# The fifth tile of each sender block holds two slot pairs instead of four slots

## The chip, the cores and the metric

One Trainium2 chip, one of its cores. The metric is the device time of one execution in microseconds (us); lower is better. A core has five engines with a queue each: PE (TensorE, matmuls), DVE (VectorE), ACT (ScalarE), POOL (GpSimd, which here issues the indirect DMAs) and SP (SyncE, which issues nearly all other DMAs). They meet through semaphores; 16 DMA engines move the data.

## The reference, cut to what matters

A graph network of four parts over 3125 nodes and 53125 edges, width 128, each part followed by a residual and a layer norm:

```python
x = layernorm(x + gated_gnn(x))     # 2 steps: msgs = (h @ edge_W[type])[src]; sum by dst; GRU
x = layernorm(x + rgcn(x))          # 3 layers: mean by (type, dst) of x[src], a weight per type, relu
x = layernorm(x + gcn(x))           # sum by src of norm[src] * norm[dst] * x[dst], one weight
x = layernorm(x + mlp(concat([x, mean_by_src(edge_attr), mean_by_dst(edge_attr)])))
```

All of it is gather by one end of an edge and sum by the other.

## The kernel before

**Slots and records.** The 25 blocks of 126 sender nodes (`TB`, `BS`) each get a run of slots, one for every edge that the block sends; an edge's slot is its rank in its block. Four slots in a row are one record of 4 x 128 floats in the DRAM tensor `chunks` (`x1_d`), and a code (target and type) for each of the four stands behind them. 128 records are a tile. A block has `QS` = 5 tiles, so `CAP` = 2560 slots, and there are `NQ` = 125 tiles.

**First loop** (52 groups of 1024 edges). It computes the first message sum and, beside it, each edge's rank: `ranks` on DVE turns a rank into a lane (`slot_lane`) and a column (`slot_col`); ACT builds the one-hot columns from `slot_col` (line 1364), DVE the lanes (`lanes_of`), and PE places the edges (line 892) in a table of slots. The ACT queue also hands POOL the row numbers of a later group (line 1344) for its gathers.

**Layers 1 to 4** (k = 1 is the second GNN step, 2 to 4 the RGCN layers) have two kinds of work. A *tile*: DVE compares the senders' lanes with the lane number (`shot`, `slot_hot`), PE multiplies it with the block's rows, one matmul a slot, four a tile (line 1030, `spread_slots`), ACT evacuates to one of `XS` = 6 buffers `xs` (line 1386, `keep_tile`), and SP stores that buffer into `chunks` (line 601, `store_tile`); before every fifth tile's store or behind it SP loads the lanes of a block three ahead. A *window* (149 of 21 target nodes): POOL gathers 128 records (line 735) into `rec`, DVE compares the codes (`dhot`), and PE sums by target and type (line 1058). In layer 1 all tiles come first, then all windows; POOL copies each tile's codes into `xs` and SP stores them with the tile. In layers 2 to 4 a plan written out by `joined` interleaves them: tiles go block by block within a round, the fourth slot group of all blocks before the fifth, so tiles 100 to 124 are the fifth tiles of the 25 blocks, the *last round*, with 36 to 38 windows between them. POOL waits for the stores of a round before the first window that needs it, and between its gathers it also scatters the edges' attributes (line 744), two in three windows of layers 3 and 4. The layers' order is fixed, so what SP issues is in the order of `store_tile`.

**GCN stage** (the last one). Now the sum goes by sender: SP loads one tile's records and its attributes into one of `GR` = 6 buffers `grec` (lines 720 and 721, two DMAs a tile, the first waits until the matmuls of the tile six before are done), DVE makes `ghot` (`slot_hots`), PE multiplies, four matmuls a tile (line 1289), and after each block of five tiles the sums are turned (`turn`, three matmuls). The tiles go block by block here, so every fifth is a fifth tile.

A float32 matmul shows in the profile as two records of the line. Layer norms, the GRU and the MLP lie between and after these stages.

## Time and profile before

| | before |
|---|---|
| timed runs, median of 3 (range) | 2967.55 us (2962.49 to 2968.0) |
| profiled execution, span | 2969.2 us |
| PE busy, share of the span | 2492.2 us (84%) |
| DVE | 1808.3 us (61%) |
| POOL | 1585.9 us (53%) |
| ACT | 868.5 us (29%) |
| stores of a tile (layer 1 / 2 to 4) | 258 KB x125 / 256 KB x375, one DMA each |
| loads of a tile in the GCN stage | 256 KB and 32 KB, x125 each |

The profile is of one execution, whose own time is its span, 1.7 us over the median of the timed ones. PE's share is an average over stages with different limits: slices of the span stand between 50% and 99% busy. In the profile's rows, a line Lnnn is a line of the kernel, x is a count, and SPq is the issue of a DMA by SP (not counted as busy time).

### The profile page before, as it was taken

What the parts mean: (1) busy time and instruction counts of PE and PEld (TensorE: products, weight loads), DVE (VectorE), ACT (ScalarE), POOL (GpSimd) and SP (SyncE); (2) the same over time, 40 slices, a digit from 0 to 9 for tenths busy, and PEclk for the clock granted to TensorE, in tenths of its full rate; (3) what the DMA queues carried; (4) which work ended last, traced back from release to release, by engine and by line L of the source; (5) the groups of instructions that cost most, each with busy time, mean ns of one, the idle gap of its engine ahead of it and who ended that gap; (6) DMA issues with size and microseconds to landing.
All of it is one profiled execution on the core that took longest, in us unless ns stands there. A gap on an engine that the chain in (4) does not pass through costs nothing.

```text
span 2969.2 us, 45704 instructions
## 1 busy us (share of the span) xinstructions
PE 2492.2 (84%) x15625; PEld 2211.7 (74%) x15625; DVE 1808.3 (61%) x6126; ACT 868.5 (29%) x1546; POOL 1585.9 (53%) x1706
## 2 busy tenths in 40 slices
PE   7587878888687899746999998998989897878798
PEld 3366666666387889436999997888988886777797
DVE  4565656575576777423876655676865554433585
ACT  2355555554354111213222231111311110443102
POOL 0656666663577666542566626666456665565200
PEclk9789888888799999857999999999999999898899
DMA  7312112110398666106888887877788774565793
GB/s 273 111 50 53 51 51 53 51 52 25 103 281 260 166 173 170 38 27 210 274 272 270 269 266 231 240 228 211 238 273 251 226 234 134 174 213 198 232 267 105
DMA packets 271515, 520.11 MB, mean 175 GB/s; under 512 B 61999, under 2 KB 115554, under 8 KB 270501
## 3 DMA queue, kind: packets, MB, share of 16 engines
q1 hardware_dynamic: 185053, 289.49, 31.2%
q0 software_dynamic: 86224, 227.59, 26.6%
q8 instruction: 132, 2.16, 0.3%
q14 instruction: 106, 0.87, 0.1%
HBM read 323.93 MB, written 192.99 MB: 174 GB/s over the span
## 4 chain that ended last, share of the span: by engine, by line
PE 69%; issue 10%; DMA 7%; DVE 6%; another core or an unknown queue 4%; ACT 2%; POOL 2%; SPq 0%; DVEq 0%; POOLq 0%; ACTq 0%
PE ps L1058 21%; PE ps L1030 10%; PE ps L892 7%; PE ps L1043 6%; PE ps L1245 5%; PE ps L1289 4%; PE ps L886 4%; PE ps L878 4%; DMA chunks<-xs 2%; DMA rec<-chunks,idx 2%; DMA srow<-lanes_of_slots 1%; DVE shot L2033 1%; POOL attributes L744 1%; PE ps L1112 1%
## 5 line engine op out<-in xcount | busy, mean ns | idle before, releaser
L735 POOL DMA_INDIRECT rec<-chunks,idx x596 | 588.5, 987 | 500.5 <-PE ps L1058 184.9
L1058 PE MATMUL ps<-dhot,rec 128*128 128x168 f32 x4768 | 757.2, 312 | 70.4 <-issue 35.3
L1058 PEld LDWEIGHTS ps<-dhot,rec 128*128 128x128 f32 x4768 | 703.8, 194 | 99.6 <-issue 77.6
L2054 DVE TENSOR_SCALAR dhot<-iota,dcode 128x168 f32<-128x168 f32 x2384 | 584.6, 311 | 216.7 <-remote 102.4
L1030 PE MATMUL ps<-hrow,shot 126*128 126x128 f32 x4000 | 516.3, 284 | 63.8 <-issue 29.5
L735 POOL DMA_INDIRECT msg<-messages,idx_buf x416 | 398.2, 957 | 307.3 <-issue 189.7
L1030 PEld LDWEIGHTS ps<-hrow,shot 126*128 126x128 f32 x4000 | 493.7, 199 | 81.7 <-issue 65.9
L1386 ACT ACTIVATE xs<-ps 128x512 f32<-128x512 f32 x500 | 295.1, 597 | 763.5 <-PE ps L1030 393.8
L744 POOL DMA_INDIRECT attributes<-w,rank_to x352 | 353.2, 1004 | 213.1 <-issue 102.2
L2033 DVE TENSOR_SCALAR shot<-srow,lane_no 126x512 f32<-126x512 uint8 x500 | 230.2, 486 | 117.4 <-PE ps L1030 51.2
L892 PE MATMUL ps<-big,lane1h 128*128 128x300 f32 x832 | 231.6, 432 | 9.3 <-issue 8.0
L836 POOL DMA_INDIRECT chunks<-xo,put_idx x149 | 148.8, 999 | 119.7 <-ACT xo L1516 80.3
L892 PEld LDWEIGHTS ps<-big,lane1h 128*128 128x128 f32 x832 | 158.6, 196 | 69.6 <-issue 24.6
L1245 PE MATMUL ps<-yrows,thot 126*128 126x128 f32 (+1 forms) x1192 | 167.1, 302 | 41.9 <-ACT xo L1516 26.4
L878 PE MATMUL ps<-onehot,msg 128*128 128x128 f32 x832 | 129.9, 294 | 84.3 <-issue 83.6
L1364 ACT ACTIVATE tmp<-iota,slot_col 128x300 f32<-128x300 f32 x416 | 186.4, 530 | 33.3 <-DVE slot_col L1701 29.6
L1245 PEld LDWEIGHTS ps<-yrows,thot 126*128 126x128 f32 (+1 forms) x1192 | 158.3, 215 | 50.0 <-ACT xo L1516 29.9
L1043 PE MATMUL ps<-agg_rows,w 128*128 128x252 f32 (+1 forms) x832 | 185.5, 374 | 8.7 <-issue 8.2
L878 PEld LDWEIGHTS ps<-onehot,msg 128*128 128x128 f32 x832 | 117.1, 206 | 93.2 <-issue 93.0
L1043 PEld LDWEIGHTS ps<-agg_rows,w 128*128 128x128 f32 x832 | 153.1, 193 | 29.9 <-issue 13.7
L1676 DVE TENSOR_SCALAR onehot<-iota,dst_lo 128x128 f32<-128x128 f32 x416 | 88.4, 297 | 126.6 <-remote 124.7
L2099 DVE TENSOR_TENSOR agg_rows<-ps,tmp 128x504 f32<-128x504 f32 (+1 forms) x150 | 100.9, 673 | 99.5 <-PE ps L1058 51.3
(304 smaller groups left out, 2538.6 us busy)
## 6 DMA issues: line engine op xcount, KB each, us to landing
chunks<-xs SPq DMA_DIRECT2D x375, 256.0 KB
tmp<-inverse_counts SPq DMA_DIRECT2D x36, 1008.0 KB
chunks<-xs SPq DMA_DIRECT2D x125, 258.0 KB
srow<-lanes_of_slots SPq DMA_DIRECT2D x100, 320.0 KB
grec<-chunks SPq DMA_DIRECT2D x125, 256.0 KB
messages<-big SPq DMA_DIRECT2D x25, 504.0 KB
trow<-lanes_of_targets SPq DMA_DIRECT2D x30, 320.0 KB
rec<-chunks,idx POOLq DMA_INDIRECT x596
```

The source lines that it names most:

```text
L735: eng.indirect_dma_start(buf, None, table, bass.IndirectOffsetOnAxis(ap=index, axis=0)).then_inc(sem, 16)
L744: eng.indirect_dma_start(attr_d, bass.IndirectOffsetOnAxis(ap=rank_to[:, c:c + 1], axis=0), attr_rows(k, n // G)[:, n % G * TC + T:(n % G ...
L878: last = mm(ps[:, g % 2, 0:P], msg[:, g % SUB, t, :], onehot[:, g % 2, t, :], start=t == 0, stop=t == G - 1)
L892: last = mm(ps[:, 7, near_col(g):near_col(g) + NEAR], lane1h[:, g % 2, t, :], big[:, g % 2, t * NEAR:(t + 1) * NEAR], start=False, stop=Fa ...
L1030: last = mm(ps[:, STAGE1_BANKS[i % 3], j * P:(j + 1) * P], shot[0:BS, i % SS, j * P:(j + 1) * P], hrow[0:BS, sb_, :], start=True, stop=True)
L1043: last = mm(out, wt(REL[k], T)[:, t * P:(t + 1) * P], agg[gi % 2][:, t, 0:c1 - c0], start=t == 0, stop=k == 1 and t == T - 1)
L1058: last = mm(ps[:, 4 + i % 2, (v % 3) * WT:(v % 3 + 1) * WT], rec[:, v % RS, j * P:(j + 1) * P], dhot[:, v % DS, j * WT:(j + 1) * WT], star ...
L1245: last = mm(ps[:, STAGE1_BANKS[v % 3], j * P:(j + 1) * P], thot[0:nodes_of(c), v % SS, j * P:(j + 1) * P], yrows[0:nodes_of(c), c, :], sta ...
L1364: last = act(away[:, t * NEAR:(t + 1) * NEAR], iota[:, near_col(g):near_col(g) + NEAR], ACT.Abs, scale=-1.0, bias=slot_col[:, g % SUB, t:t ...
L1386: act(xs[:, i % XS, 0:4 * P], ps[:, STAGE1_BANKS[i % 3], :], ACT.Copy).then_inc(q("x1_evac"), 1)
L2033: vec.tensor_scalar(shot[0:BS, i % SS, :], srow[0:BS, s_ % NS, (n % QS) * SPAN:(n % QS + 1) * SPAN], lane_no1[0:BS], None, ALU.is_equal).t ...
L2054: last = vec.tensor_scalar(dhot[:, v % DS, j * WT:(j + 1) * WT], iota[:, 0:WT], dcode[:, v, j:j + 1], None, ALU.is_equal)
```

## The change

A block's fifth tile becomes half a tile. It has 128 lanes but two slots a lane (`slot_cols`): lane l of the lower half and lane 64 + l of the upper half together are the four slots of one record. So a block has 576 records (`BLOCK_RECS`) and 2304 slots instead of 2560, and the fifth tile costs two matmuls, half the one-hot columns and half an evacuation. Its store in layers 2 to 4 is two DMAs of 64 partitions (slots 0 and 1 from the lower lanes, slots 2 and 3 from the upper), in layer 1 four, since the codes are no longer beside the slots. In the GCN stage each half of the partitions loads whole rows of the 64 records, the upper half from two slots further on, so that both halves find their two slots in the same columns; the attributes come in two DMAs as well. `ranks` gets six more small operations in the groups that can hold ranks of 2048 and over, the last 12 of 52. `slot_wait` for the stores becomes `put_wait`, which counts one, two or four DMAs a tile. The other edits (the order of the slot table's columns, its size of 450 columns, its store from 113 partitions instead of 125, clears and reads of matching width) follow from this.

```diff
@@ -49,11 +49,15 @@
 SPAN = 512
 QS = 5
 NQ = TB * QS
-NTILE = NQ * 4
+FULL = NQ - TB
 QCOLS = 4 * TB
+NTILE = 4 * FULL + 2 * TB
+LANE_ROWS = -(-NTILE // 4)
 NEAR = 3 * QCOLS
 NEAR_STEPS = (24, 40)
-CAP = QS * SPAN
+HALF = P // 2
+BLOCK_RECS = (QS - 1) * P + HALF
+CAP = 4 * BLOCK_RECS
 WD = 21
 WT = WD * T
 NW = -(-NODES // WD)
...
-RECS = NQ * P
+RECS = TB * BLOCK_RECS
 RS, DS, SS, XS, NS = 6, 4, 4, 6, 3
...
@@ -416,9 +421,34 @@
 
             return buf[:, first:first + YW * (NYB - 2) + 1:YW]
 
-        def tile_slots(i):
-
-            return (i % QS) * QCOLS + i // QS * 4
+        def slot_cols(n):
+
+            return 4 if n < FULL else 2
+
+        def first_col(n):
+
+            return 4 * n if n < FULL else 4 * FULL + 2 * (n - FULL)
+
+        def by_record(i):
+
+            return i % QS * TB + i // QS
+
+        def first_record(n):
+
+            return n % TB * BLOCK_RECS + n // TB * P
+
+        def puts(k, n):
+
+            return 1 if n < FULL else 4 if k == 1 else 2
+
+        def all_puts(s, runs):
+
+            return sum(puts(k, n) for k in range(1, runs + 1) for n in range(s, NQ, XS))
+
+        def put_wait(eng, k, i):
+
+            s = i % XS
+            eng.wait_ge(q(f"x1_stored_{s}"), 16 * (all_puts(s, k - 1) + sum(puts(k, n) for n in range(s, i + 1, XS))))
 
         def targets_got(eng, c):
 
@@ -428,7 +458,8 @@
         def record_got(eng, i):
 
             s = i % GR
-            eng.wait_ge(q(f"x1_stored_{s}"), 16 * (4 * len(range(s, NQ, XS)) + 2 * (i // GR + 1)))
+            loads = sum(1 if by_record(n) < FULL else 2 for n in range(s, i + 1, GR))
+            eng.wait_ge(q(f"x1_stored_{s}"), 16 * (all_puts(s, 4) + 2 * loads))
 
         def record_put(eng, v):
...
@@ -573,8 +604,9 @@
 
             def lanes_load(k, s):
 
-                eng.dma_start(srow[:, s % NS, :],
-                              srow_d[s * QS * 4:(s + 1) * QS * 4, :].rearrange("c p -> (c p)").partition_broadcast(P))\
+                c0, c1 = first_col(s * QS), first_col((s + 1) * QS)
+                eng.dma_start(srow[:, s % NS, 0:(c1 - c0) * P],
+                              srow_d[c0:c1, :].rearrange("c p -> (c p)").partition_broadcast(P))\
                    .then_inc(q(f"lanes_loaded_{s % NS}"), 16)
 
...
@@ -596,10 +628,20 @@
                     after(eng, "x1_evac", k, i + 1)
                     if k == 1:
                         eng.wait_ge(q("code_put"), i + 1)
-                    cols = RECORD_COLS if k == 1 else 4 * P
-                    at = (n % TB * QS + n // TB) * P
-                    eng.dma_start(x1_d[at:at + P, 0:cols], xs[:, i % XS, 0:cols])\
-                       .then_inc(q(f"x1_stored_{i % XS}"), 16)
+                    at = first_record(n)
+                    if n < FULL:
+                        cols = RECORD_COLS if k == 1 else 4 * P
+                        eng.dma_start(x1_d[at:at + P, 0:cols], xs[:, i % XS, 0:cols])\
+                           .then_inc(q(f"x1_stored_{i % XS}"), 16)
+                    else:
+                        for z in range(2):
+                            lanes, to = slice(z * HALF, (z + 1) * HALF), slice(2 * z * P, 2 * (z + 1) * P)
+                            eng.dma_start(x1_d[at:at + HALF, to], xs[lanes, i % XS, 0:2 * P])\
+                               .then_inc(q(f"x1_stored_{i % XS}"), 16)
+                            if k == 1:
+                                codes = slice(4 * P + 2 * z, 4 * P + 2 * z + 2)
+                                eng.dma_start(x1_d[at:at + HALF, codes], xs[lanes, i % XS, 4 * P:4 * P + 2])\
+                                   .then_inc(q(f"x1_stored_{i % XS}"), 16)
                     ahead = n // QS + NS - 1
                     if k >= 3 and n in (20, 25, 30):
                         for s in {20: (), 25: (6,), 30: (7, 8)}[n]:
...
@@ -717,9 +759,18 @@
             for i in range(NQ):
                 if i >= GR:
                     eng.wait_ge(q("gcn_sum"), i - GR + 1)
-                eng.dma_start(grec[:, i % GR, 0:4 * P], x1_d[i * P:(i + 1) * P, 0:4 * P]).then_inc(q(f"x1_stored_{i % GR}"), 16)
-                eng.dma_start(grec[:, i % GR, 4 * P:], attr_d[i * 4 * P:(i + 1) * 4 * P, :].rearrange("(p j) a -> p (j a)", j=4))\
-                   .then_inc(q(f"x1_stored_{i % GR}"), 16)
+                at, to = first_record(by_record(i)), grec[:, i % GR, :]
+                if by_record(i) < FULL:
+                    eng.dma_start(to[:, 0:4 * P], x1_d[at:at + P, 0:4 * P]).then_inc(q(f"x1_stored_{i % GR}"), 16)
+                    eng.dma_start(to[:, 4 * P:], attr_d[4 * at:4 * (at + P), :].rearrange("(p j) a -> p (j a)", j=4))\
+                       .then_inc(q(f"x1_stored_{i % GR}"), 16)
+                else:
+                    attrs = attr_d[4 * at:4 * (at + HALF), :].rearrange("(l z j) a -> z l (j a)", z=2, j=2)
+                    for z in range(2):
+                        lanes = slice(z * HALF, (z + 1) * HALF)
+                        eng.dma_start(to[lanes, 0:4 * P - 2 * A * z], x1_d[at:at + HALF, 2 * A * z:4 * P])\
+                           .then_inc(q(f"x1_stored_{i % GR}"), 16)
+                        eng.dma_start(to[lanes, 4 * P:4 * P + 2 * A], attrs[z]).then_inc(q(f"x1_stored_{i % GR}"), 16)
             eng.wait_ge(q("gcn_added"), NCH)
             eng.wait_ge(q("turn_used"), NCH)
             general(GCN)
...
@@ -792,8 +843,9 @@
                 send_attrs(1, n)
             for i in range(NQ):
                 if i >= XS:
-                    slot_wait(eng, "x1_stored", XS, 1, NQ, i - XS)
-                eng.tensor_copy(xs[:, i % XS, 4 * P:RECORD_COLS], code[:, 4 * i:4 * i + 4]).then_inc(q("code_put"), 1)
+                    put_wait(eng, 1, i - XS)
+                eng.tensor_copy(xs[:, i % XS, 4 * P:4 * P + slot_cols(i)], code[:, first_col(i):first_col(i) + slot_cols(i)])\
+                   .then_inc(q("code_put"), 1)
                 if i % 2 == 0:
                     send_attrs(1, AT_FIRST[1] + i // 2)
...
@@ -1026,7 +1079,7 @@
                 elif k >= 3:
                     after(eng, "x1_evac", k - 1, NQ)
                 after(eng, "shot", k, i + 1)
-                for j in range(4):
+                for j in range(slot_cols(tile_no(k, i))):
                     last = mm(ps[:, STAGE1_BANKS[i % 3], j * P:(j + 1) * P], shot[0:BS, i % SS, j * P:(j + 1) * P],
                               hrow[0:BS, sb_, :], start=True, stop=True)
                 last.then_inc(q("stage1_mm"), 1)
...
@@ -1284,10 +1337,11 @@
                     eng.wait_ge(q("sums_kept"), b - 1)
                 eng.wait_ge(q("ghot"), i + 1)
                 record_got(eng, i)
-                for j in range(4):
+                cols = slot_cols(by_record(i))
+                for j in range(cols):
                     got = grec[:, i % GR, :].rearrange("p (m s a) -> p s m a", s=4, a=A)[:, j]
                     last = mm(ps[0:BS, 6 + b % 2, 0:P + A], ghot[:, i % GH, j, :], got, start=first_tile and j == 0,
-                              stop=last_tile and j == 3)
+                              stop=last_tile and j == cols - 1)
                 last.then_inc(q("gcn_sum"), 1)
                 if i % QS == 2 and b >= 1:
...
@@ -1380,10 +1434,11 @@
                 def keep_tile(k, i):
                     after(eng, "stage1_mm", k, i + 1)
                     if i >= XS:
-                        slot_wait(eng, "x1_stored", XS, k, NQ, i - XS)
+                        put_wait(eng, k, i - XS)
                     elif k >= 3:
-                        slot_wait(eng, "x1_stored", XS, k - 1, NQ, range(i, NQ, XS)[-1])
-                    act(xs[:, i % XS, 0:4 * P], ps[:, STAGE1_BANKS[i % 3], :], ACT.Copy).then_inc(q("x1_evac"), 1)
+                        put_wait(eng, k - 1, range(i, NQ, XS)[-1])
+                    cols = slot_cols(tile_no(k, i)) * P
+                    act(xs[:, i % XS, 0:cols], ps[:, STAGE1_BANKS[i % 3], 0:cols], ACT.Copy).then_inc(q("x1_evac"), 1)
 
                 def keep_sums(k, gi):
                     after(eng, "xf_mm", k, gi + 1)
...
@@ -1694,10 +1749,26 @@
                                              ALU.bitwise_and))
                     st.did(vec.tensor_scalar(rank_i[:, 2, :], rank_i[:, 0, :], 9, None, ALU.arith_shift_right))
                     st.did(vec.tensor_scalar(rank_i[:, 3, :], rank_i[:, 0, :], 3, None, ALU.bitwise_and))
+                    last_round = g >= NEAR_STEPS[-1]
+                    if last_round:
+                        st.did(vec.tensor_scalar(rank_i[:, 4, :], rank_i[:, 0, :], 1, 1, ALU.arith_shift_right,
+                                                 ALU.bitwise_and))
+                        st.did(vec.tensor_scalar(rank_half[:, 0, :], ranks_g, float(4 * P * (QS - 1)), None, ALU.is_ge))
                     st.settle()
-                    st.did(vec.tensor_copy(slot_lane[:, g % SUB, :], rank_i[:, 1, :]))
-                    st.do(vec.scalar_tensor_tensor(out=rank_hi[:], in0=rank_i[:, 2, :], scalar=float(QCOLS),
-                                                   in1=rank_i[:, 3, :], op0=ALU.mult, op1=ALU.add))
+                    st.did(vec.scalar_tensor_tensor(out=rank_hi[:], in0=rank_i[:, 2, :], scalar=float(QCOLS),
+                                                    in1=rank_i[:, 3, :], op0=ALU.mult, op1=ALU.add))
+                    if last_round:
+                        st.did(vec.tensor_tensor(rank_half[:, 1, :], rank_half[:, 0, :], rank_i[:, 4, :], ALU.mult))
+                        st.did(vec.tensor_tensor(rank_half[:, 0, :], rank_half[:, 0, :], src_sb[:, g * G:(g + 1) * G], ALU.mult))
+                        st.settle()
+                        st.did(vec.scalar_tensor_tensor(out=slot_lane[:, g % SUB, :], in0=rank_half[:, 1, :],
+                                                        scalar=float(HALF), in1=rank_i[:, 1, :], op0=ALU.mult, op1=ALU.add))
+                        st.do(vec.tensor_tensor(rank_half[:, 0, :], rank_half[:, 0, :], rank_half[:, 1, :], ALU.add))
+                        st.do(vec.scalar_tensor_tensor(out=rank_hi[:], in0=rank_half[:, 0, :], scalar=-2.0, in1=rank_hi[:],
+                                                       op0=ALU.mult, op1=ALU.add))
+                    else:
+                        st.did(vec.tensor_copy(slot_lane[:, g % SUB, :], rank_i[:, 1, :]))
+                        st.settle()
                     vec.scalar_tensor_tensor(out=slot_col[:, g % SUB, :], in0=src_sb[:, g * G:(g + 1) * G], scalar=4.0,
                                              in1=rank_hi[:], op0=ALU.mult, op1=ALU.add).then_inc(q("slot_known"), 1)
 
...
@@ -2030,11 +2102,12 @@
                         after(eng, "stage1_mm", k - 1, NQ)
                     if k >= 2:
                         st.settle()
-                    vec.tensor_scalar(shot[0:BS, i % SS, :], srow[0:BS, s_ % NS, (n % QS) * SPAN:(n % QS + 1) * SPAN],
+                    cols = slot_cols(n) * P
+                    vec.tensor_scalar(shot[0:BS, i % SS, 0:cols], srow[0:BS, s_ % NS, (n % QS) * cols:(n % QS + 1) * cols],
                                       lane_no1[0:BS], None, ALU.is_equal).then_inc(q("shot"), 1)
                     if k == (4 if s_ < 8 else 2 if s_ < 16 else 3):
                         after(eng, "shot", k, i + 1)
-                        st.did(vec.tensor_reduce(deg_part[0:BS, n:n + 1], shot[0:BS, i % SS, :], AX.X, ALU.add))
+                        st.did(vec.tensor_reduce(deg_part[0:BS, n:n + 1], shot[0:BS, i % SS, 0:cols], AX.X, ALU.add))
                     if k == 1 and i in beside:
                         what, args = beside[i]
                         what(*args)
```

SP's queue in the GCN stage, from where buffers come round again. Before:

```order
L720 DMA grec<-chunks 128x512 [waits gcn_sum]
L721 DMA grec<-attributes 128x64
L720 DMA grec<-chunks 128x512 [waits gcn_sum]
L721 DMA grec<-attributes 128x64
L720 DMA grec<-chunks 128x512 [waits gcn_sum]
L721 DMA grec<-attributes 128x64
```

Now, with the end of one block and the start of the next:

```order
L764 DMA grec<-chunks 128x512 [waits gcn_sum]
L765 DMA grec<-attributes 128x64
L771 DMA grec<-chunks 64x512 [waits gcn_sum]
L773 DMA grec<-attributes 64x32
L771 DMA grec<-chunks 64x480
L773 DMA grec<-attributes 64x32
L764 DMA grec<-chunks 128x512 [waits gcn_sum]
L765 DMA grec<-attributes 128x64
```

A block's five tiles now take 12 issues where they took 10.

SP's queue in layer 1, where the last round begins. Before (the last row holds the last 14 tiles):

```order
L576 DMA srow<-lanes_of_slots 128x2560
L601 DMA chunks<-xs 128x516 [waits code_put,x1_evac] x5
L576 DMA srow<-lanes_of_slots 128x2560
L601 DMA chunks<-xs 128x516 [waits code_put,x1_evac] x5
L576 DMA srow<-lanes_of_slots 128x2560
L601 DMA chunks<-xs 128x516 [waits code_put,x1_evac] x14
```

Now:

```order
L634 DMA chunks<-xs 128x516 [waits code_put,x1_evac] x4
L639 DMA chunks<-xs 64x256 [waits code_put,x1_evac]
L643 DMA chunks<-xs 64x2
L639 DMA chunks<-xs 64x256
L643 DMA chunks<-xs 64x2
L608 DMA srow<-lanes_of_slots 128x1280
L639 DMA chunks<-xs 64x256 [waits code_put,x1_evac]
L643 DMA chunks<-xs 64x2
L639 DMA chunks<-xs 64x256
L643 DMA chunks<-xs 64x2
```

Each of the 25 tiles takes four issues where it took one.

PE in the last round of layer 2 (1030 and 1083 are tiles, 1058 and 1111 window sums). Before:

```order
L1030 MATMUL ps<-hrow,shot 128x128 x8
L1058 MATMUL ps<-dhot,rec 128x168 x12
L1030 MATMUL ps<-hrow,shot 128x128 x8
L1058 MATMUL ps<-dhot,rec 128x168 x12
L1030 MATMUL ps<-hrow,shot 128x128 x8
```

Now, at the same place:

```order
L1083 MATMUL ps<-hrow,shot 128x128 x4
L1111 MATMUL ps<-dhot,rec 128x168 x12
L1083 MATMUL ps<-hrow,shot 128x128 x4
L1111 MATMUL ps<-dhot,rec 128x168 x12
L1083 MATMUL ps<-hrow,shot 128x128 x4
```

The order stays; each tile has half its matmuls.

## Rows read from the trace of the kernel before

**Rows 1.** Six stretches: us; busy PE, PEld, DVE, ACT, POOL (instructions); clock, DMA, GB/s

```profile
597.00:749.00 152.00, 130.08 (x676) 104.74 (x676) 96.48 (x400) 76.94 (x132) 69.58 (x72) 0.89 0.14 37
935.00:972.00 37.00, 22.69 (x181) 20.80 (x179) 10.33 (x24) 14.49 (x25) 24.50 (x45) 0.92 0.82 247
1593.00:1671.00 78.00, 78.00 (x563) 76.69 (x563) 52.34 (x182) 16.12 (x28) 51.51 (x52) 1.00 0.89 268
1974.00:2066.00 92.00, 84.65 (x547) 81.25 (x545) 68.25 (x204) 15.19 (x27) 61.89 (x62) 0.93 0.76 225
2372.00:2466.00 94.00, 84.53 (x543) 78.52 (x541) 52.54 (x184) 15.63 (x27) 63.26 (x64) 0.96 0.75 222
2779.00:2923.00 144.00, 139.94 (x1075) 130.04 (x1075) 115.53 (x545) 3.65 (x7) 0.00 (x0) 0.98 0.89 257
```

**Rows 2.** Timeline of ACT, last round of layer 1: start, us, what [idle before <-releaser]

```profile
934.90 0.60 ACT L1386 ACTIVATE xs<-ps 128x512 f32<-128x512 f32 x1 [0.60 <-DMA chunks<-xs]
...
962.12 0.60 ACT L1386 ACTIVATE xs<-ps 128x512 f32<-128x512 f32 x1 [0.86 <-PE ps L1030]
```

**Rows 3.** Chain of the GCN stage: start us, us, what; then SP's waits there

```profile
2782.18 9.62 PE ps L1289 x64
...
2808.80 5.10 PE ps L1289 x40
...
2814.32 5.09 PE ps L1289 x40
...
2919.34 2.17 PE ps L1289 x16
...
SPq L720 <- PE ps L1289: 28.4, 89, 1.1
```

**Rows 4.** Timeline of SP's DMA issues in the GCN stage: start us, us, what

```profile
2779.23 0.32 SPq L720 DMA_DIRECT2D grec<-chunks  x1
2779.60 0.43 SPq L721 DMA_DIRECT2D grec<-attributes  x1
2780.08 0.42 SPq L720 DMA_DIRECT2D grec<-chunks  x1
2780.55 0.43 SPq L721 DMA_DIRECT2D grec<-attributes  x1
...
2856.52 1.40 SPq L721 DMA_DIRECT2D grec<-attributes  x1
```

**Rows 5.** Timeline of SP's issues of other shapes, elsewhere

```profile
748.21 0.32 SPq L685 DMA_DIRECT2D lanes_of_slots<-dhot  x1
...
777.98 0.28 SPq L690 DMA_DIRECT2D lists<-dhot  x1
778.30 0.26 SPq L691 DMA_DIRECT2D lists<-dhot  x1
...
1708.47 0.43 SPq L582 DMA_DIRECT2D tmp<-inverse_counts  x1
```

**Rows 6.** Timeline of PE in the last round of layer 2

```profile
1601.31 1.95 PE L1030 MATMUL ps<-hrow,shot 126*128 126x128 f32 x16
1603.10 3.59 PE L1058 MATMUL ps<-dhot,rec 128*128 128x168 f32 x24
```

**Rows 7.** POOL's groups in the layer-4 window: busy, mean ns, idle before

```profile
L735 POOL DMA_INDIRECT rec<-chunks,idx x38 | 38.4, 1009 | 21.8 <-remote 9.6 <-issue 8.5 <-PE ps L1058 3.6
L744 POOL DMA_INDIRECT attributes<-w,rank_to x26 | 25.7, 987 | 7.9 <-issue 7.9
```

**Rows 8.** Timeline of DVE in loop group 46; then POOL's waits, 597 to 749 us

```profile
663.12 0.17 DVE L1695 TENSOR_SCALAR rank_i<-rank_i 128x8 int32<-128x8 int32 x1
663.20 0.17 DVE L1696 TENSOR_SCALAR rank_i<-rank_i 128x8 int32<-128x8 int32 x1
663.39 0.17 DVE L1698 CAST slot_lane<-rank_i 128x8 f32<-128x8 int32 x1
...
POOL msg L735 <- ACT idx_buf L1344: 21.7, 6, 5.1
```

35 lines of the change are left out of this document (19 added, 16 removed).

## The prediction, on record before the result

> **What bounds the kernel now.** I read the busy times of the whole span first (the small table above: PE stands far ahead), then those of the stretches in which the change does something [rows 1], and then, for each stretch, what the engine on the chain waits for. An average over the span says little here: the change touches stretches with different limits, so each needs its own sum. What the reader is to see in them:
>
> - Last round of layer 1 (tiles 100 to 124 alone, no window sums beside them). ACT evacuates tile 100 at 934.90 us and tile 124 at 962.12 us, 27.2 us for 24 tiles, 1.13 us a tile; ACT waits here for the stores of earlier tiles to land [rows 2]. PE is busy 22.7 of 37 us and the DMA engines 0.82 of it [rows 1]. Transfers bound it, not PE.
> - Last round of layer 2. PE is busy 78.00 of 78 us at full clock [rows 1]: PE bounds it without a gap.
> - Last rounds of layers 3 and 4. 92 and 94 us with PE busy 84.7 and 84.5 at granted clocks 0.93 and 0.96, and POOL with 62 and 64 issues [rows 1]. PE mostly bounds, POOL stands close behind.
> - GCN stage (the last stage). PE runs 40 matmul records in 5.10 us, block after block, and SP waits for PE before a tile's first load, 28.4 us in 89 waits [rows 3]. PE bounds it; but SP's own work for a tile is two issues, and back to back they start 0.47 us apart [rows 4], so SP needs 0.95 us of the 1.02 us that a tile's eight matmul records take (8 x 5.10 / 40). The second limit is 7% away, and that is what decides this prediction.
>
> **The price of an issue on SP.** The change turns one DMA of 128 partitions into two or four of 64. The trace shows no DMA of 64 partitions. The nearest rows: 2 KB a partition and 256 B a partition both go at 0.47 us from start to start (2779.60, 2780.08, 2780.55) [rows 4]; a load of inverse counts, 128 partitions in 8 runs each, takes 0.43 us to issue as well [rows 5]. So neither bytes nor runs set the price. Only the list stores, 25 partitions, are cheaper: 0.32 us from 777.98 to 778.30 [rows 5]. Upper bound 0.475 us, lower bound, on a straight line between 25 and 128 partitions, 0.32 + 39/103 x 0.155 = 0.38 us. I take 0.475: the rows in which size varies eightfold do not move at all, while the cheap ones, besides being few partitions, are an odd number of them. The 0.38 is kept as a rival.
>
> **The change part by part**, against the span of 2969.2 us of the profiled execution (the median of the timed runs is 2967.55 us, 1.7 us less; I carry differences over to it).
>
> Layer 1, last round. Removed: two of four matmuls a tile and half the bytes; both lie beside the transfers. Added: a tile's store is now four issues (two of records, two of codes), with a fifth of a lane load beside it. SP a tile: 4 x 0.475 + 0.475 / 5 = 2.0 us, against 1.13 us for the whole tile before. Transfers get lighter and hide under it; SP becomes the bound. 24 x (2.0 - 1.13) = **+21 us**, less 1 us since the last store lands in a quieter queue: **+20 us**. With 0.38 us an issue: 1.6 us a tile, **+10 us**. Queued behind SP here: the store of inverse counts, for which ACT waits before the first window sum, and POOL's first gather, which waits for the last six stores. So it all lies on the path. PE is then busy 0.45 of every 2.0 us and may begin the sums at half clock; the sums after it would pay 1 to 2 us. I add **+1.5 us**.
>
> The rule for this edit in the Trainium skill, page "DMA: Bandwidth & Descriptors", section "Rules for kernel authors": two transfers to disjoint partition halves serialize over the same engines, so one 128-partition transfer is to be preferred. It speaks against the change in the same direction as the rows; by it alone the halves cost nothing but their issue.
>
> Layers 2 to 4, last rounds. Removed: 50 matmuls a layer, each two records. In the dense stretch, 16 records of the tile form start at 1601.31 and the next form starts at 1603.10 [rows 6]: 1.79 / 16 = 0.112 us. 100 x 0.112 = 11.2 us a layer, if nothing else is late next. SP: two issues a tile and a lane load, about 1.1 us of some 3 us: hidden. DVE (one-hot rows half as wide) and ACT (evacuation half as wide) only gain, and had room. Next in line is POOL: in the layer-4 window its 64 issues take 64.1 us busy and 16.4 us between them [rows 7], so it needs 80.5 of 94 us, and by the same 1.26 us an issue 78 of 92 in layer 3 and 66 of 78 in layer 2 [rows 1]. Layer 2: 78 - 11.2 = 66.8, just above POOL's 66: **-10.5 us**. Layer 3: floor 78, and PE's own gaps are in part waits for POOL's gathers: **-8 us** of 11.2. Layer 4, PE at the end of longer waits: **-6 us**. Bounds: -33.6 us together if PE alone counts, -15 us if the waits take half. I take -24.5 us.
>
> GCN stage. Removed: 50 matmuls; a block of five tiles falls from 40 to 36 records, 5.52 (5.10 and the transposes) to 5.0 us [rows 3]. Added on SP: four loads for the fifth tile instead of two, 12 issues a block: 12 x 0.475 = 5.7 us, more than PE's 5.0 and than the 5.52 of before. The records' bytes are unchanged (64 rows twice, whole). SP now sets the end: 300 x 0.475 = 142.5 us, and the issues that take 1.4 us instead of 0.43 [rows 4], 7 in the stage before, add 7 us: 149.5 us. Before, SP's first issue was at 2779.23 and the last tiles were summed at 2919.34 + 2.17 = 2921.5 us [rows 3, 4]. After: 2779.2 + 149.5 + some 2.5 us from issue to use (2779.60 to 2782.18, the first matmul [rows 3, 4]) = 2931.2 us: **+9.5 us**. With 0.38 us: 200 x 0.475 + 100 x 0.38 + 7 = 140, **0 us**; the bound from below is PE's 36 records, 25 x 0.52 = **-13 us**.
>
> First loop, the last 12 of 52 groups. Added on DVE: six small operations net, of 0.17 us, those that wait for one another 0.2 us apart and the others 0.08 [rows 8]: about 0.85 us a group before ACT can build its tables. ACT's next step hands POOL its indices, and POOL waits for that 21.7 us in six waits in this stretch [rows 8]. Fully on the path: +10 us; fully hidden, since PE is busy 130 of 152 us [rows 1]: 0. PE is nearer to the bound, so I take **+2 us**.
>
> Costed at nothing: the lane store of 113 rows instead of 125 (issued at 748.21, and not needed before the lists that go out at 777.98 [rows 5]: 30 us of cover), a memset of two columns, and fewer clears of the attribute table, all under GRU work or the loop.
>
> **Sum:** 2 + 20 + 1.5 - 10.5 - 8 - 6 + 9.5 = +8.5 us. 2967.5 + 8.5 = **2976 us**.
>
> **Rivals.**
> 1. *An issue of 64 partitions costs less* (0.38 us). For it: 25 partitions cost 0.32. Against: sizes change nothing at 128. Layer 1 +10, no clock loss, GCN 0: 2 + 10 - 24.5 = -12.5, **2955 us**, faster. It decides both SP stretches at once.
> 2. *POOL and the loop take back what PE gives*, the mechanism that makes it clearly slower: POOL's queue behind PE in layers 3 and 4 gives only -4 instead of -14, and the DVE chain in the loop costs 10 instead of 2. +8.5 + 10 + 8: **2994 us**. It holds once POOL's issues a layer stand above 1.3 us each. For it: 21.7 us of POOL's waits behind ACT; against: PE's full window in layer 2.
> 3. *Issue time does not count, transfers and PE do.* Layer 1 then gains with the bytes, of which about half are gone: at 0.6 to 0.7 us a tile about -10 us, GCN -12, layers -24.5, loop +2: -44.5 in all, **2923 us**. The rows speak against it: SP fills 0.95 of 1.02 us a tile already [rows 3, 4]. The Trainium skill, same page, section "Issuing engines are not separate DMA queues", says that issue time is usually small relative to the DMA itself; this rival is that rule.
> 4. *The change does not do what it says*, for example waits on more increments than come early. A tile's semaphore needs all its stores, which SP sends in one go, so I see no more than is in the sum.
>
> **How the numbers follow.** Forecast 0.58 (2958 to 2990, by the bounds of layers and loop), rival 1 0.20, rival 2 0.15, rival 3 0.04, the rest 0.03. A measurement of this kernel can tell about 0.2% (6 us) from no change: faster is below 2961.6, slower above 2973.5. The forecast's own range puts 0.61 of it above, 0.34 between, 0.05 below; rival 1 puts three quarters below and the rest between. Faster: 0.03 + 0.15 + 0.04 = 0.22; the same: 0.20 + 0.05 = 0.24; slower 0.54. The range 2948 to 2994 leaves out rival 3 and the outer parts of rivals 1 and 2, under 2 in 10.
>
> **What would show it.** In the GCN stage SP's issues run without gaps, 0.47 us apart for 64 partitions too, PE waits for loads, and the stage is near 150 us long from SP's first issue (SP's waits for PE gone). In layer 1 the last 24 tiles take 48 us, 2.0 us each. In layer 2 the window from tile 100 to 124 falls from 77 to 66 us with PE still full. If issues of 64 partitions start 0.38 us apart or less, the prediction is wrong in rival 1's direction; if the layer-3 and 4 windows hardly shrink and POOL's waits for PE vanish, in rival 2's.

## The result, and the profile of the changed kernel

The changed kernel takes 3044.96 us (median of 4 runs, 3042.21 to 3049.68) against 2967.78 us of the kernel before beside it (2962.49 to 2978.29): a ratio of 1.0249, 95% interval 1.0217 to 1.028. It is slower, as forecast, but by 77 us and not by 8.5, and outside the range. The profiled executions have spans of 3041.0 and 2969.2 us; these 71.8 us are accounted for here.

Where they lie, from ACT's evacuations of the first, the hundred-first and the last tile of each layer (the tiles of [rows 2]) and DVE's one-hots in the last stage:

| stretch | before, us | changed, us | difference | forecast |
|---|---|---|---|---|
| start to first tile of layer 1 | 808.8 | 819.7 | +10.9 | +2 |
| layer 1, tiles 0 to 100 | 126.1 | 126.3 | +0.2 | 0 |
| layer 1, tiles 100 to 124 | 27.2 | 51.9 | +24.7 | +20 |
| from there to layer 2 | 391.6 | 393.9 | +2.3 | +1.5 |
| layer 2, last round | 76.8 | 74.0 | -2.8 | -10.5 |
| layer 3, last round | 92.0 | 91.0 | -1.0 | -8 |
| layer 4, last round | 94.2 | 89.4 | -4.8 | -6 |
| the rest of layers 2 to 4 | 849.5 | 856.9 | +7.4 | 0 |
| layer 4's last tile to first one-hot | 302.4 | 309.3 | +6.9 | 0 |
| one-hots of the last stage and tail | 200.5 | 228.7 | +28.1 | +9.5 |

The stretches of [rows 1] in the changed kernel, in the same columns; loop, last rounds of layers 1 to 4, last stage:

```profile
597.00:749.00 152.00, 125.77 (x669) 102.25 (x668) 97.75 (x455) 76.73 (x131) 72.42 (x76) 0.88 0.15 39
946.00:998.00 52.00, 23.43 (x92) 18.48 (x91) 6.00 (x20) 9.32 (x25) 19.04 (x40) 0.56 0.35 80
1633.00:1708.00 75.00, 70.66 (x465) 66.26 (x464) 50.24 (x183) 10.69 (x28) 49.47 (x50) 1.00 0.82 226
2014.00:2105.00 91.00, 73.72 (x446) 65.67 (x445) 60.45 (x207) 10.09 (x27) 59.45 (x61) 0.98 0.67 183
2413.00:2503.00 90.00, 77.41 (x440) 69.79 (x439) 47.42 (x176) 9.90 (x27) 58.36 (x59) 0.90 0.68 181
2823.00:2993.00 170.00, 140.77 (x969) 120.51 (x970) 107.37 (x492) 3.49 (x6) 0.00 (x0) 0.98 0.78 214
```

In layer 1's last round the DMA engines fell from 0.82 to 0.35 busy and TensorE's clock from 0.92 to 0.56 (half speed, 1.2 GHz, for most of it): nothing is full any more except SP. Its timeline there, and the chain of waits of the same stretch:

```profile
960.47 0.60 SPq L643 DMA_DIRECT2D chunks<-xs  x1
961.11 0.60 SPq L639 DMA_DIRECT2D chunks<-xs  x1
961.75 0.60 SPq L643 DMA_DIRECT2D chunks<-xs  x1
962.38 0.59 SPq L608 DMA_DIRECT2D srow<-lanes_of_slots  x1
```

```profile
by line: SPq L643 44.7%; SPq L639 42.4%; issue 8.5%; SPq L608 3.4%; ACT xs L1441 1.5%; SPq L630 0.6%; ACTq L451 0.0%
```

L639 stores a half's records (64 partitions of 1,024 bytes), L643 its codes (64 of 8 bytes). An issue of either starts 0.64 us before the next, whatever it carries (the first of a tile 0.49 to 0.59 us); 0.475 was the most I had allowed. Four of them and a fifth of a lane load make 2.7 us a tile. The 24.7 us by which ACT's last evacuation came later understate it, since ACT runs six buffers ahead of SP: GpSimd's first gather, which waits for the last stores, came 32.8 us after tile 100's evacuation before and 68.2 us after it now.

```profile
946.01 0.38 ACT L1441 ACTIVATE xs<-ps 128x256 f32<-128x256 f32 x1 [0.32 <-DMA chunks<-xs]
...
997.89 0.38 ACT L1441 ACTIVATE xs<-ps 128x256 f32<-128x256 f32 x1 [1.89 <-DMA chunks<-xs]
```

```profile
1014.16 0.98 POOL L786 DMA_INDIRECT rec<-chunks,idx  x1 [13.74 <-DMA chunks<-xs]
```

The last stage shows the same. SP's timeline, where [rows 4] had one issue every 0.475 us (L764 and L765 are the loads of a full tile, L771 and L773 those of a half), and SP's waits there, 12.5 us in place of the 28.4 us of [rows 3]:

```profile
2867.47 0.45 SPq L771 DMA_DIRECT2D grec<-chunks  x1
2867.97 0.60 SPq L773 DMA_DIRECT2D grec<-attributes  x1
2868.61 0.60 SPq L771 DMA_DIRECT2D grec<-chunks  x1
2869.24 0.60 SPq L773 DMA_DIRECT2D grec<-attributes  x1
2869.88 0.58 SPq L764 DMA_DIRECT2D grec<-chunks  x1
2870.51 0.43 SPq L765 DMA_DIRECT2D grec<-attributes  x1
...
2873.84 0.45 SPq L771 DMA_DIRECT2D grec<-chunks  x1
```

```profile
SPq L764 <- PE ps L1343: 10.0, 23, 1.1
SPq L771 <- PE ps L1343: 2.5, 7, 0.5
```

From one fifth tile to the next SP needs 2873.84 - 2867.47 = 6.37 us, against TensorE's 5.52 us a block before. Its 300 issues run from 2823.0 to 2988.7 us, 165.7 us with hardly a gap; the 250 of before took 136.2 us, of which 25 us were gaps. The first load of the full tile behind a half one, over 128 partitions, takes 0.63 us as well (2869.88 to 2870.51), so a half tile also makes the issue behind it dearer.

### The profile page after: what moved, and what is told of

Read it like the earlier page. It is cut to its first block, busy times and chain, and to the rows that moved or that the text cites. A ratio compares the mean times of both kernels' runs of the same rounds, so it can differ in the third digit from the quotient of the medians.

```text
span 3041.0 us, 44927 instructions
## 1 busy us (share of the span) xinstructions
PE 2481.6 (82%) x15125; PEld 2174.2 (71%) x15125; DVE 1789.9 (59%) x6149; ACT 846.4 (28%) x1546; POOL 1586.7 (52%) x1706
## 4 chain that ended last, share of the span: by engine, by line
PE 56%; DVE 12%; issue 8%; another core or an unknown queue 8%; DMA 7%; SPq 4%; ACT 2%; POOL 2%; DVEq 0%; POOLq 0%; ACTq 0%
PE ps L1111 21%; PE ps L1083 10%; PE ps L1096 5%; PE ps L1298 5%; PE ps L945 3%; DMA rec<-chunks,idx 2%; DVE lane1h L1779 2%; PE ps L939 2%; PE ps L1343 2%; PE ps L931 2%; DMA chunks<-xs 2%; DMA grec<-attributes 2%; DVE onehot L1731 1%; POOL rec L786 1%
## 5 line engine op out<-in xcount | busy, mean ns | idle before, releaser
L1111 PE MATMUL ps<-dhot,rec 128*128 128x168 f32 x4768 | 768.9, 314 | 106.4 <-issue 51.4
L1083 PE MATMUL ps<-hrow,shot 126*128 126x128 f32 x3600 | 486.2, 288 | 90.8 <-ACT xs L1441 32.8
L1083 PEld LDWEIGHTS ps<-hrow,shot 126*128 126x128 f32 x3600 | 459.1, 202 | 112.7 <-issue 64.3
L1441 ACT ACTIVATE xs<-ps 128x512 f32<-128x512 f32 (+1 forms) x500 | 272.4, 554 | 778.0 <-PE ps L1083 365.6
L2106 DVE TENSOR_SCALAR shot<-srow,lane_no 126x512 f32<-126x512 uint8 (+1 forms) x500 | 217.3, 462 | 129.9 <-DMA srow<-lanes_of_slots 65.1
L945 PEld LDWEIGHTS ps<-big,lane1h 128*128 128x128 f32 x832 | 158.4, 196 | 68.4 <-issue 24.7
L931 PE MATMUL ps<-onehot,msg 128*128 128x128 f32 x832 | 136.4, 303 | 76.5 <-issue 73.9
L931 PEld LDWEIGHTS ps<-onehot,msg 128*128 128x128 f32 x832 | 121.0, 212 | 89.8 <-issue 89.4
L2172 DVE TENSOR_TENSOR agg_rows<-ps,tmp 128x504 f32<-128x504 f32 (+1 forms) x150 | 100.9, 673 | 129.0 <-PE ps L1111 71.8
L1096 PEld LDWEIGHTS ps<-agg_rows,w 128*128 128x128 f32 x832 | 152.5, 192 | 25.3 <-issue 9.9
```

Of the source, the lines that this page charges most:

```text
L931: last = mm(ps[:, g % 2, 0:P], msg[:, g % SUB, t, :], onehot[:, g % 2, t, :], start=t == 0, stop=t == G - 1)
L945: last = mm(ps[:, 7, near_col(g):near_col(g) + NEAR], lane1h[:, g % 2, t, :], big[:, g % 2, t * NEAR:(t + 1) * NEAR], start=False, stop=Fa ...
L1083: last = mm(ps[:, STAGE1_BANKS[i % 3], j * P:(j + 1) * P], shot[0:BS, i % SS, j * P:(j + 1) * P], hrow[0:BS, sb_, :], start=True, stop=True)
L1096: last = mm(out, wt(REL[k], T)[:, t * P:(t + 1) * P], agg[gi % 2][:, t, 0:c1 - c0], start=t == 0, stop=k == 1 and t == T - 1)
L1111: last = mm(ps[:, 4 + i % 2, (v % 3) * WT:(v % 3 + 1) * WT], rec[:, v % RS, j * P:(j + 1) * P], dhot[:, v % DS, j * WT:(j + 1) * WT], star ...
L1441: act(xs[:, i % XS, 0:cols], ps[:, STAGE1_BANKS[i % 3], 0:cols], ACT.Copy).then_inc(q("x1_evac"), 1)
```

## The experiments

Each run is compared with the kernel before on the same chip. The chips are not alike: E1 to E4, E9 to E12, and E13 with E14 ran on three chips where the kernel before takes 2647, 2644 and 2644 us, E5 to E8 on one where it takes 2971 us, like the first pair. Stretches are compared within one of these two kinds, each from one profiled execution: E3 and E14, both the kernel before, differ by 0 to 2 us in the stretches of the table under E1 and E2. Of the some 320 us between the kinds 142 lie ahead of layer 1 (666.7 us to its first tile, not 808.8), 75 between layer 1's last tile and layer 2, the rest in the later stretches. The slower chip's profiles have hundreds of us of gaps on ScalarE and VectorE that end at queues the profile does not know, the faster chips' none; why the chips differ is open.

### E5: the changed kernel once more

> The changed kernel itself once more, on the chip of the runs beside it. Price theory (64 partitions 0.64 us an issue, as the tail measured on a machine with nothing else to do): against the kernel before it stands at a ratio of 1.015 to 1.025, with tiles 100 to 124 of layer 1 at about 52 us against 28 and the last stage's one-hots at about 180 us from the first to the last against 155. Rival (the loss came from the execution recorded first, in which part of the idle time ends at unknown queues): ratio below 1.008.

3031.12 us (3022.99 to 3039.25), ratio 1.0217 (1.0137 to 1.0297); tiles 100 to 124 of layer 1 in 51.9 us, one-hots in 175.2 us. The loss repeats. The first tile came at 803.0 us here, 799.7, 802.5 and 822.1 in its neighbours E7 (unchanged loop), E6 and E8 (three more small operations in the loop). On this chip the stretch scatters by 20 us and can't tell the loop term; on the faster chips it is 0 to 3 us (below), E8's loop included, so most of the +10.9 of the first pair was chance.

### E3: the price by itself

```
+ for n in (128, 127, 125, ..., 8):                     # behind the last store
+     probe(8 loads xs[0:n, 256 columns] <- chunks[n rows])   # 8 issues, then wait for all
```

> The kernel before with a tail behind its last store: on SP's queue, with nothing else under way, series of eight transfers of equal shape between DRAM and SBUF, each series awaited before the next: 128, 127, 125, 120, 113, 112, 96, 80, 72, 65, 64, 63, 60, 56, 48, 32, 25, 16 and 8 partitions of 1,024 bytes, then 64, 32 and 16 partitions from partition 64 on, then 128, 64 and 32 partitions of 128 and of 8 bytes, stores of 128, 64 and 32 partitions, and loads of 2,048 bytes for 128 and 64. Price theory: the distance between two issues depends on the number of partitions alone, 0.475 us at 128 and 0.64 at 64 also on an idle machine, for lower and upper half, load and store, 8 and 1,024 bytes alike. Rival (the 0.64 us is SP being held up by the traffic of the layer or by a full ring): alone, 64 partitions take no longer than 128, 0.24 to 0.475 us.

With nothing else under way, one group a series (the first two of eight left out): duration of an issue in ns, least, median, most. 128, 127, 65, 64 and 63 partitions of 1,024 bytes:

```profile
L735 SPq DMA_DIRECT2D xs<-chunks x6: 432/432/433, 2639.1 to 2641.5; - x6
L735 SPq DMA_DIRECT2D xs<-chunks x6: 5491/5632/5635, 2645.9 to 2674.1; - x6
...
L735 SPq DMA_DIRECT2D xs<-chunks x6: 372/372/373, 2772.4 to 2774.4; - x6
L735 SPq DMA_DIRECT2D xs<-chunks x6: 596/597/597, 2777.6 to 2780.8; - x6
L735 SPq DMA_DIRECT2D xs<-chunks x6: 322/322/323, 2783.9 to 2785.7; - x6
```

From start to start it is 0.04 us more: 0.475 us at 128, 0.416 at 65, **0.639 at 64**, 0.365 at 63, 0.449 at 60, 0.412 at 72, 0.46 to 0.47 at 16, 32, 48, 80, 96 and 112. Sixty-four is dear from partition 64 on as well, as a store, with 8, 128 or 2,048 bytes. So the traffic of the kernel has no part in it, nor bytes or direction: the price theory holds and its rival falls. The first issue of a series, after a pause, is cheaper (0.50 to 0.55 us at 64, 0.37 at 128). At 127 and 113 an issue takes 5.6 and 5.0 us from the third of a series on. By the Trainium skill, page "DMA: Bandwidth & Descriptors", section "Why a DMA increments its semaphore by 16 and not by 1", the number of DMA engines is the largest up to 16 that divides the partitions, one for a prime like 127; the series fits it (5.6 us an issue at 127, 0.39 at 125). The same divisor sorts the prices: E3 and E14 together give 0.46 to 0.475 us where it is 16 (128, 112, 96, 80, 48, 32, 16 partitions), 0.45 where it is 15 (120, 60), 0.41 where it is 12 (72, 36, 24), 0.39 to 0.40 where it is 11 (88, 66, 44) and 0.365 at 63 (9). Below that it does not (125 and 25, both 5, cost 0.39 and 0.34), and 64 falls out altogether: its divisor is 16 and its price 0.639.

### E1 and E2: the two stretches apart

```
E1 (last stage)                                   E2 (stores of the fifth tiles)
- for z in range(2): to[lanes z] <- 64 rows       - for z in range(2): 64 rows <- xs[lanes z] (, codes)
+ to[:, ...] <- 128 rows; attributes 128 x 32     + 64 records, as 128 halves <- xs[:, 0:258 or 256]
```

> The changed kernel with one part altered: in the last stage a fifth tile is loaded by two transfers over all 128 partitions (128 rows of 2,048 bytes, then 128 rows of attributes) in place of four over 64. Half of the rows are then the wrong ones, so the sums of that stage are not the reference's; the number of matmuls and waits is unchanged. Price theory (an issue over 64 partitions costs SP 0.64 us against 0.475 for 128, and SP's queue is what the last stage waits for, 300 issues of 152.7 us): a block of five tiles falls from 6.37 us back to about the 5.52 of the kernel before, so the time falls by 22 to 35 us, to 3010 to 3023. Rival (the stage is long because half tiles leave the DMA engines badly filled or the one-hots of VectorE come late, not because of SP): the 128 rows bring even more bytes, the blocks stay above 6.2 us and the time above 3038.

> The changed kernel with the stores of the fifth tiles altered: each is one transfer of 128 partitions (258 columns in layer 1, 256 later), laid into the same 64 records, in place of four (layer 1) or two (later) over 64 partitions. The halves of a record are then shuffled and the codes misplaced, so the output is not the reference's. Price theory: in layer 1's last round SP issues 25 transfers in place of 100 at 0.64 us, and tiles 100 to 124 fall from 51.9 us to about 27 or a little less: 20 to 28 us gained there, and up to 5 more in the last rounds of layers 2 to 4; time 3012 to 3025. Rival (the round is long because TensorE stands at half clock or ScalarE and GpSimd hand over late): those give no more than 5 us, time above 3038.

E1 2663.98 us, ratio 1.0059 (1.0038 to 1.0079); E2 2657.1 us, ratio 1.0048 (1.0028 to 1.0068), beside the changed kernel's 1.0217 to 1.0249. The changed kernel itself did not run on this kind of chip; each of the two shows what the other's stretch costs there (worked out from them, E1 with E2's last stage would stand at 2664 + 34 = 2698 us, a ratio of 1.019). The stretches that were altered, in one table with the other runs of this kind of chip (E3 holds the kernel before; the last stage is first to last one-hot):

| us | before (E3) | E1 | E2 | E4 | E10 | E11 | E13 |
|---|---|---|---|---|---|---|---|
| layer 1, tiles 100 to 124 | 27.9 | 52.2 | 21.5 | 29.3 | 29.2 | 38.1 | 23.0 |
| layer 2, last round | 74.0 | 63.3 | 65.3 | 64.8 | 64.5 | 65.5 | 64.6 |
| layer 3, last round | 77.2 | 76.8 | 77.1 | 76.2 | 64.7 | 65.5 | 64.6 |
| layer 4, last round | 78.6 | 75.9 | 77.6 | 76.3 | 64.2 | 64.3 | 64.0 |
| last stage | 155.2 | 145.8 | 179.9 | 151.1 | 150.9 | 155.4 | 150.2 |

E1 takes 34 us from the last stage and leaves layer 1 at 52 us; E2 takes 31 us from layer 1 and leaves the last stage at 180 us. The two losses are separate and both are SP's. E2's last round of layer 1 came out at 21.5 us, below the 27 that was expected and the 27.9 of before: it stores half the bytes with one issue a tile. E1's last stage is 9 us below the kernel before; the 50 matmuls less of this stage are the likely reason, which no run isolates.

### E6: one number

```
- HALF = P // 2
+ HALF = 63
```

> The changed kernel with one number altered: half tiles hold 63 records, not 64 (the blocks still fit), so every transfer of a half goes over 63 partitions. The tail measured 0.365 us for an issue over 63 and 0.64 over 64. Price theory: a fifth tile's four stores in layer 1 take SP 1.46 us in place of 2.56, tiles 100 to 124 fall from 52 to about 36 us; in the last stage SP needs 1.46 in place of 2.5 us, which puts the blocks back at the 5.5 us of the DMA engines: 15 us gained in layer 1, 20 to 27 in the last stage, together 33 to 45 us against the changed kernel. Rival (the cost is the half transfer itself: more packets of 1,024 bytes and fewer DMA engines at work on one of them): 63 partitions spread over fewer engines, so the time stays or rises.

2971.08 us, ratio 1.0015 (0.9976 to 1.0055), 60 us below E5 beside it: more than the 33 to 45 expected. Layer 1's last round took 31.9 us, the one-hots 152.5 us. SP's timeline in the last stage, to be read against that above:

```profile
2795.76 0.35 SPq L771 DMA_DIRECT2D grec<-chunks  x1
2796.15 0.32 SPq L773 DMA_DIRECT2D grec<-attributes  x1
2796.51 0.32 SPq L771 DMA_DIRECT2D grec<-chunks  x1
2796.88 0.32 SPq L773 DMA_DIRECT2D grec<-attributes  x1
```

The same number of transfers, matmuls and waits, and nearly the same bytes; only the price differs (and the matmuls of a half tile read 126 lanes, not 128). This is the strictest of the runs: in the profiles 20 us come from layer 1's last round and 23 from the last stage. Another 8 lie between layer 4 and the one-hots (302.8, 311.1 in E5) and 9 in the first hundred tiles of layer 1 (125.6, 134.5 in E5), for which I have no cause.

### E4: halves in pairs of lanes

```
- lane = record + 64 z;  2 x (64 rows <- xs[64 lanes]), 2 x codes
+ lane = 2 record + z;   chunks[64 rows, "r (z c) -> r z c"] <- xs[:, 0:256], once; codes once
```

> The changed kernel with another placing inside a half tile: lane 2r+z of the tile holds half z of record r (the placing computes it with three more small operations of VectorE in the loop's last twelve groups), so a half tile is stored by one transfer over 128 partitions with two 1,024-byte runs per record, plus one for the codes in layer 1, and loaded in the last stage by one of 128 runs of 1,920 bytes and one of attributes. The table of lanes is stored from 120 partitions, not 113. Price theory: SP needs 0.95 us for a fifth tile in layer 1 (2.56 in the changed kernel), 0.475 in layers 2 to 4 (1.28), 0.95 in the last stage (2.2 to 2.5). Layer 1 gains 15 to 25 us, the last stage 30 to 40, the store of the lanes 0 to 4, layers 2 to 4 0 to 6: 2968 to 2995, near the kernel before or up to 1% above it. Rival (half tiles cost time in another way than by SP's issues): above 3010.

2638.75 us, ratio **0.9969** (0.9953 to 0.9985): a little faster than the kernel before, where the changed kernel was over 2% slower, and better than the 1.000 to 1.009 expected. Its single transfers still took 0.52 to 0.60 us each, though they go over 128 partitions.

### E7 to E10: why layers 3 and 4 gave nothing

In the table above layer 2's last round gained 9 to 11 us, as forecast; layers 3 and 4 gained 0 to 3. Layer 3's last round, in E3 (the kernel before) and E4, in the columns of [rows 1], and GpSimd's two groups in E4:

```profile
1729.00:1806.00 77.00, 74.91 (x535) 72.78 (x534) 66.69 (x201) 15.73 (x27) 58.99 (x60) 1.00 0.88 261
```

```profile
1731.00:1807.00 76.00, 67.05 (x436) 62.28 (x435) 58.99 (x201) 10.45 (x27) 58.03 (x60) 1.00 0.80 216
```

```profile
L784 POOL DMA_INDIRECT rec<-chunks,idx x36 | 35.4, 985 | 11.0 <-issue 9.4 <-PE ps L1109 1.5
L793 POOL DMA_INDIRECT attributes<-w,rank_to x24 | 24.1, 1006 | 7.3 <-issue 7.3
```

TensorE's busy time drops by 7.9 us and the stretch by 1. GpSimd has 60 operations: 59.5 us busy and 16.7 us in gaps between one and the next in which it waits for nothing that the profile shows ("issue" in the rows), 76.2 of 76 us. It was full before too, just beside TensorE. So I took sends away from it, in two steps, each in the kernel before and in E4:

```
E7, E8: AT_FIRST = {..., 3: 26, 4: 26}; one send with every gather below 24, then with every third
E9, E10: the same, then with every second: about 5 of 88 sends are left in the last round, of 24
```

> The kernel before with the attribute sends of layers 3 and 4 moved on GpSimd's queue: 26 of the 88 of each layer stand ahead of its first gather, 24 among the first 24 gathers, the other 38 one to every third gather (two to three from the twelfth on before). The attributes are loaded at the fifteenth tile. Reason for it: in the last rounds of layers 3 and 4 GpSimd's queue is full in both kernels (60 operations of 1.28 us in 77 us), so a saving of TensorE there can't show. Queue theory: TensorE is busy 75 of those 77 us here too, so this kernel gains little, 0 to 6 us in all. Rival (GpSimd is not what these rounds wait for): within 2 us of the kernel before, and e8 gains no more than this one.

> The kernel with paired halves (e4_pairs) and the same move of the attribute sends as in e7. Queue theory: with GpSimd out of the way the 50 matmuls less of a fifth-tile round show, as they did in layer 2 (65 us in place of 74): 6 to 9 us gained in each of layers 3 and 4 beyond what e7 gains, ratio to the kernel before 0.989 to 0.993. Rival (DMA landings or ScalarE set these rounds): the ratio stays at the 0.997 of e4_pairs plus what e7 shows.

> The kernel before with GpSimd's queue relieved further: in layers 3 and 4, 26 attribute sends ahead of the first gather, 24 among the first 24 gathers and the other 38 one to every second gather, so that about two are left in the last round (13 in e7_early_before, 24 before). It is the pair of e10. TensorE is busy the whole last round here, so nothing is expected against e7: last rounds of layers 3 and 4 at 72 to 75 us, ratio to the kernel before 0.991 to 0.996.

> The paired halves with the same order of sends as e9. In e8 the last rounds still took 76.2 and 73.6 us with TensorE busy 68 to 72 of them and 48 to 51 operations on GpSimd at a mean distance of 1.5 us. Queue theory (GpSimd's own rate still set them): with 38 operations they fall to TensorE's 66 to 69 us, 5 to 8 us below e9 in each of the two layers, ratio to the kernel before 0.986 to 0.991. Ring theory (the six record buffers: free, gather issued, landed, multiplied, some 11.7 us for six windows): they stay at 72 to 76 us, like layer 2's, whatever GpSimd does.

E7: ratio 0.9939 (0.9906 to 0.9971), E8: 0.9927 (0.9883 to 0.997), last rounds 74.1 and 73.4 us in E7, 76.3 and 73.6 in E8. Both gained, E7 more than the 0 to 6 us expected, but the pair did not part: E8's ratio lies in its range by E7's gain, and the 6 to 9 us a layer that it was to gain beyond E7 did not come. On the first pair's chip, of the same kind, the kernel before had needed 92 and 94 us for the 61 and 63 operations of these rounds, which is where E7's gain comes from (the rounds ahead lost 11 to 12 us a layer). In E7 TensorE fills the last rounds; in E8 it is busy 71.8 and 67.5 us of them, and GpSimd's 48 to 51 operations stand 1.5 us apart on average (1.3 at the median) with gaps that mostly end at TensorE's window sums, not at unknown queues (layer 3, then layer 4):

```profile
POOL rec L784 <- PE ps L1109: 11.7, 11, 1.6
POOL rec L784 <- remote: 2.8, 2, 1.4
...
POOL rec L784 <- PE ps L1109: 10.7, 10, 2.2
POOL rec L784 <- remote: 3.6, 2, 1.8
```

GpSimd's rate alone does not explain E8, then, and why the saving fails to show on this chip stays open. E9 and E10 ran on a faster one. With 43 operations, 38 of them gathers (E9, then E10; layers 3 and 4 each):

```profile
1740.00:1814.00 74.00, 74.00 (x537) 72.81 (x536) 66.64 (x205) 15.75 (x27) 42.43 (x43) 1.00 0.92 273
2102.00:2178.00 76.00, 74.46 (x539) 73.03 (x538) 52.47 (x181) 15.76 (x27) 41.87 (x43) 1.00 0.92 266
```

```profile
1741.00:1806.00 65.00, 64.03 (x443) 62.38 (x442) 56.72 (x199) 10.65 (x28) 41.50 (x43) 1.00 0.91 254
2095.00:2160.00 65.00, 64.51 (x446) 62.91 (x445) 48.80 (x181) 10.64 (x27) 41.37 (x43) 1.00 0.91 258
```

E9 2640.21 us, ratio 0.9991 (0.9973 to 1.001); E10 2618.29 us, ratio **0.9891** (0.9868 to 0.9915). TensorE is full in both, and the round is 9.3 and 11.6 us shorter: all of the saving shows. The 11.2 us a layer that I had priced were about right; what stood beside TensorE was not counted as a second bound at the same height. The condition "GpSimd free" makes the difference of the two kernels, not the sends as such: in E9 alone they bought nothing, against an expected ratio of 0.991 to 0.996, since the 3 us that each last round gained on E3 were paid for in the rounds ahead (278.4 and 278.6 us from tile 0 to tile 100 of layers 3 and 4, 270.3 and 273.8 in E3).

### E12: is it the ring of buffers?

```
- RS, DS, SS, XS, NS = 6, 4, 4, 6, 3
+ RS, DS, SS, XS, NS = 5, 4, 4, 6, 3
```

> e10 with five record buffers in place of six (the ring of the scatter stage, which shares the number, has five too). Ring theory: the last rounds of layers 2 to 4 are held by the time from a buffer's release to its next multiplication, so they grow by up to a fifth, from 73 to 80 to 88 us. Queue theory (GpSimd's rate or TensorE): less than 2 us in each.

2672.21 us, ratio 1.0099 (1.008 to 1.0119). The last rounds grew to 68.0, 68.4 and 69.3 us, by 3.5 to 5: neither the fifth that a ring at its limit would give nor nothing. The kernel as a whole lost 54 us against E10: in the profiles 22 us lie between layer 1's last tile and layer 2, where the window sums run, and 23 in the rest of layers 2 to 4. So the ring is at most a small part of what held E10's last rounds (TensorE is full there), but five buffers are too few, above all outside these rounds; whether a seventh would still gain was not tried.

### E11, E13, E14: which form of a transfer is dear

```
E11: E10 with HALF = 60        E13: E10, the codes of all half tiles in 2 transfers ahead of layer 1
```

> e10 with half tiles of 60 records (120 lanes) in place of 64. In e4 and e8 SP still paid 0.56 to 0.64 us for the paired transfers of 64 records by 2; the tail gave 0.45 us for 60 partitions and 0.64 for 64. Price theory (it is the 64 in a transfer's outer size that is dear, also with 128 partitions): 0.45 to 0.48 us an issue; tiles 100 to 124 of layer 1 fall from 29 to 22 to 25 us and the last stage's one-hots from 148 to 142 to 147 us: 5 to 12 us below e10. Rival (the price hangs on the number of packets): no difference from e10.

> e10_last_free_pairs with the codes of the 25 half tiles taken out of the tiles' stores: two transfers of 64 partitions by 25 runs of 8 bytes, issued once before the lists of the windows are awaited, in place of 25 small ones in layer 1's last round. Price theory: a half tile then costs SP one issue of 0.56 to 0.64 us in layer 1, not two; tiles 100 to 124 fall from 29 to about 22 us as in e2_store_wide (21.5), nothing else moves: 4 to 8 us below e10, ratio to the kernel before 0.986 to 0.989. Rival (the 3,200 runs of 8 bytes hold up the lists behind them on SP's queue): tile 0 starts later by as much as is gained.

> A second tail behind the kernel before's last store, series of eight loads each awaited: 126, 124, 104, 88, 76, 68, 66, 62, 61, 52, 44, 40, 36 and 24 partitions of 1,024 bytes; then DRAM sides of two sizes, r rows in z runs: 64 by 2, 63 by 2, 60 by 2, 56 by 2, 48 by 2, 32 by 2, 32 by 4, 30 by 4 and 16 by 8; then stores of 64 by 2 and 32 by 4. It asks what rule the price follows. Theory of engines (the price grows with the number of DMA engines that a transfer is split over, 0.34 at 8 or fewer to 0.475 at 16, and 64 is one exception): 62 and 61 (two and one engine) wait for the engines like 127, 68 and 66 cost 0.40 to 0.42, the two-sized forms cost by r times z, except 64 by 2 at 0.56 and 60 by 2 at 0.83. Rival (a two-sized side costs by itself): all of them lie at 0.55 to 0.85.

E11, meant to be cheaper, took 2635.85 us, ratio 0.9968 (0.9956 to 0.998), 17.6 us above E10: its paired issues take 0.83 us each and layer 1's last round 38.1 us. My reading that a 64 in the outer size is what costs fell with it. E14 shows the groups 64 by 2, 60 by 2 and 32 by 4 (rows by runs, 128, 120 and 128 partitions):

```profile
L735 SPq DMA_DIRECT2D xs<-chunks x6: 605/606/607, 2758.2 to 2761.4; - x6
...
L735 SPq DMA_DIRECT2D xs<-chunks x6: 819/820/820, 2775.0 to 2779.3; - x6
...
L735 SPq DMA_DIRECT2D xs<-chunks x6: 603/603/605, 2806.2 to 2809.5; - x6
```

Start to start: 0.64 to 0.65 us for 64, 48 and 32 rows by 2, 32 by 4 and 16 by 8; 0.78 to 0.86 for 63, 60 and 56 by 2 and 30 by 4; plain 66 and 68 partitions 0.39 and 0.37, and 61 2.5 to 3.3 us. So of the nine forms tried, a DRAM side that lays the partitions out as rows by runs costs 0.64 us, more where its outer size is no multiple of 16, and a plain side 0.34 to 0.475, except at 64, which costs what a two-sized one does. E14's theory of engines holds for the plain sides but for 64, its rival for the two-sized ones (48 by 2 costs 0.64 and not the 0.47 of 96). Several runs within each partition are another case: the load of inverse counts took the usual 0.43 us [rows 5]. Why plain 64 is dear is open: one could think that it is cut in two on its way, but no run shows it.

E13 beats all others: 2603.32 us (2602.13 to 2610.24), ratio **0.9846** (0.9829 to 0.9862), a little below the 0.986 to 0.989 expected, with layer 1's last round at 23.0 us and the first tile no later (669.9 us; 669.8 in E14, whose loop is the old one). It keeps the change's half tiles and pays for each with one issue in a layer and two in the last stage. Its edit also takes GpSimd's copy of a half tile's codes out of layer 1, and it ran on another chip than E10, so the 12 us between the two ratios are not all the issue's: 6.2 us lie in the last round of layer 1.

## Why the prediction was wrong, point by point

- **The price of an issue.** This step decides both of SP's stretches. The text took 0.475 us as its upper bound from rows at 128 and 25 partitions, as if the price lay on a line between them. It does not: 0.365 at 63, 0.639 at 64, 0.416 at 65 (E3). Nor was it so that "only the list stores" were cheaper: L720 in [rows 4] starts 0.37 us before the next over 128 partitions, after a pause, so a start-to-start distance hangs on what the queue did before too. The range had no case in which the price was above 0.475, and its inner bounds do not add up: with the bounds that the text gives for layers and loop, 2976 - 9.1 - 2 and 2976 + 9.5 + 8, it is 2965 to 2994 and not 2958 to 2990. With 0.64 (and 0.50 for the first of a half tile, as the last stage's rows show), the sum's own formula gives the last stage 200 x 0.475 + 25 x 2.42 + 7 = 162.5 us of issues, 13 us more than the 149.5 of the text; the dearer issue behind each half tile adds 25 x 0.15 = 4 us, and measured were 165.7. For layer 1 it gives 2.7 us a tile, 24 x (2.7 - 1.13) = 38 us; the first gather came 35.3 us later. E6, one number away, took the loss back.
- **Layer 1.** The mechanism was right (SP back to back, transfers lighter, clock at half). Size: +27.0 us up to layer 2 instead of +21.5. The window sums that follow gave some 8 of the 35 us back (first gather to layer 2: 386.0 us before, 377.6 now); I have not traced how. On the faster chips they gave nothing back: 309.7 us in E3, 312.1 in E1, where the first gather came 34.1 us later, so there all of it went through, as the text had it.
- **Last stage.** "SP now sets the end" was right, its waits for PE went from 28.4 to 12.5 us. Size: +28.1, not +9.5. E1 puts the whole of it on the half tiles' loads, E6 on the price of their issues.
- **Layers 2 to 4.** -24.5 was forecast; -8.6 in the last rounds, taken back by +7.4 elsewhere in these layers (-3 to +4 on the faster chips; no run isolates it). The failed step is the reading of "PE mostly bounds, POOL stands close behind". The text put POOL's need at 78 of 92 us and let 8 of 11.2 us through. On the faster chips both are full at 77 us in E3, and E3 and E4, E9 and E10 show that the saving is worth 1 to 2 us with GpSimd full and 9 to 12 us with it free. On the chip of the first pair the step failed too, but less is shown of why: PE's busy time in layer 3's window fell by 10.9 us (84.65 to 73.72) and the round by 1.0. Of the 14 us that the text took for POOL's slack, 10.0 were waits whose releaser the profile does not know, and they did not shrink (layer 3, before and changed):

```profile
POOL rec L735 <- remote: 10.0, 7, 1.7
POOL rec L786 <- remote: 12.3, 8, 2.1
```

E7 and E8, the pair on such a chip, differ by 0 to 2 us the wrong way in spite of fewer sends. That layer 2 gave 2.8 us here and 9 to 11 us on the other chips is open in the same way.
- **Loop.** +2 was forecast. On one chip the first tile comes at 669.1 to 669.6 us with the new loop (E1, E2, E4) and at 666.7 with the old, on a second at 668.7 to 670.3 (E10 to E12) and 667.5 (E9); E13 and E14 are 0.1 us apart. It is 0 to 3 us; the +10.9 of the first pair is not the change's.
- **Layer 4's end to the one-hots**, not costed in the text: +6.9 us, and 8 in E5 against E6, but 0 to 4 on a faster chip (267.6 in E3, 268.1, 269.4, 271.8). No run isolates it.
- **The rivals.** The first (a cheaper issue) fell at once. The second named the right place for the layers, but its condition, GpSimd's issues above 1.3 us each, tells nothing: on average they stand 1.49 and 1.51 us apart in layers 3 and 4 of the changed kernel, and 1.48 and 1.47 in the kernel before. Nor did it have the size of the rest; its loop term of 10 us did not come. The Trainium skill's rule in "Rules for kernel authors" on two disjoint partition halves spoke for 128-partition transfers, on the ground of the shared engines; the runs bear the advice out for another reason, SP's issue. Its section "Issuing engines are not separate DMA queues" calls issue time usually small beside the transfer; here 0.64 us of issue moved 64 KB, and it set the end of two stages.

## What to carry to other kernels

Where the queue that issues transfers is nearly as busy as the engine that uses them, count issues times their own price, and measure that price for the exact shape: a tail of eight equal transfers behind the kernel's end tells it in one run, and the price of an unmeasured shape can lie above that of all its neighbours. Halving a tile halves bytes and matmuls but not issues; lay the halves so that one transfer moves both, and take small side data out of the per-tile stores (E13). Before crediting an engine's saving, look for the second queue that is full at the same height, and test the saving with that queue relieved in both kernels.

## What the runs showed of the hardware

- An SP issue of 64 plain partitions takes 0.64 us from start to start, against 0.365 at 63 and 0.416 at 65, the same for 8 to 2,048 bytes a partition, for loads and stores, for the lower and the upper partitions, and in the kernel as on an idle queue (E3, changed kernel). After a pause it takes 0.50 to 0.55 us; a 128-partition issue right behind it 0.63.
- Plain sides with the same largest divisor up to 16 cost the same where it is 11 or more: 0.46 to 0.475 us (16), 0.45 (15), 0.41 (12), 0.39 to 0.40 (11); 64 alone falls out (E3, E14).
- A transfer whose DRAM side lays the partitions out as rows by runs takes 0.64 to 0.65 us even over 128 partitions, and 0.78 to 0.86 when the outer size is 63, 60, 56 or 30 (E14); E11's stores of 60 by 2 stood 0.88 us apart in the kernel.
- With 127, 113 or 61 partitions SP is held 2.5 to 5.7 us an issue from the third or fourth of a series on (E3, E14).
- In the last rounds of layers 3 and 4 GpSimd's gathers and sends stand, with some 60 of them in a round, 1.25 us apart at best and 1.28 to 1.29 at the median on both kinds of chip; the mean is 1.29 to 1.32 us on the faster and 1.47 to 1.51 on the slower. TensorE's full last rounds took 74.0 us on a faster chip and 74.1 on the slower in layer 3 (E9, E7), but 74.0 and 76.7 in layer 2.
